# Cross attention: turning the probabilities in 32x32 blocks on VectorE and through DRAM, with the gather two batches later

## What is computed

```python
def _L0_xattn_ref(x, z, Wq, Wkv, Wo):        # x: 64 x 32 x 512 (after a layernorm), z: 64 x 257 x 256
    Q = (x @ Wq.T).reshape(B, xN, NUM_HEADS, HEAD_DIM)
    KV = (z @ Wkv.T).reshape(B, zN, 2, NUM_HEADS, HEAD_DIM)
    K = KV[:, :, 0]
    V = KV[:, :, 1]
    attn = jnp.einsum('bqhd,bkhd->bhqk', Q, K) * SCALE
    attn = jax.nn.softmax(attn, axis=-1)
    O = jnp.einsum('bhqk,bkhd->bqhd', attn, V).reshape(B, xN, DIM)
    return O @ Wo.T
...
x = x + _L0_xattn_ref(_layernorm(x, axis=-1), ctx_512, ...)
x = x + _L0_attn_ref(_layernorm(x, axis=-1), ...)
x = x + _L0_ffn_ref(_layernorm(x, axis=-1), ...)
```

## Time and profile before

| | us |
|---|---|
| three timed runs | 1493.66, 1495.41, 1495.46 |
| median | 1495.41 |
| span of the profiled execution | 1492.9 |
| loop of the cross attention within it | from 32.2 to 687 |

### The profile page before, as it was taken

One profiled execution on the slowest core, in us unless ns is written; L12 is line 12 of the kernel. 1 busy time (PEld: TensorE's weight loads), 2 busy tenths in 40 slices (PEclk: granted clock), 3 DMA queues, 4 the chain that ended last, 5 costly groups with the idle time before them and its releaser, 6 DMA issues. The chain is left out here.

```text
span 1492.9 us, 39481 instructions
## 1 busy us (share of the span) xinstructions
PE 1434.5 (96%) x14944; PEld 1281.3 (86%) x14944; DVE 1088.6 (73%) x1945; ACT 807.5 (54%) x1525; POOL 543.6 (36%) x810
## 2 busy tenths in 40 slices
PE   7999999999999999998999998799999999999998
PEld 6888888988888888887778786698999999999997
DVE  3676777767777677776667686797887878787785
ACT  4666666666666666654434434345555545555452
POOL 1222222221222222224866876453333333333232
PEclk9999999999999999999999999899999999999999
DMA  6301101000001100100011014179877878787871
GB/s 239 125 28 31 30 22 29 29 22 29 22 28 28 29 28 23 30 9 1 31 38 38 32 38 155 57 220 314 281 263 247 286 253 267 262 279 238 292 256 44
DMA packets 130734, 174.11 MB, mean 117 GB/s; under 512 B 16953, under 2 KB 89337, under 8 KB 130626
## 3 DMA queue, kind: packets, MB, share of 16 engines
q1 hardware_dynamic: 120242, 145.56, 30.1%
q0 software_dynamic: 10384, 27.05, 5.0%
HBM read 157.18 MB, written 19.06 MB: 118 GB/s over the span
## 5 line engine op out<-in xcount | busy, mean ns | idle before, releaser
L2229 DVE TENSOR_TENSOR split<-raw,split 128x1024 fp32r<-128x1024 f32 x204 | 242.3, 1220 | 7.2 <-ACT split L2169 6.0
L52 PE MATMUL bank<-split_xT,split 128*128 128x256 f32 x768 | 216.5, 282 | 0.4 <-DVE split L2229 0.2
L54 PE MATMUL bank<-split_xT,split 128*128 128x256 f32 x768 | 215.4, 281 | 0.0
L53 PE MATMUL bank<-split_xT,split 128*128 128x256 f32 x768 | 215.4, 280 | 0.0
L2169 ACT CAST split<-raw 128x1024 fp32r<-128x1024 f32 x202 | 203.2, 1048 | 6.9 <-DMA raw<-in_L_ffn_W_dram 3.2
L596 ACT ACTIVATE Pr<-xa_s,nmax 128x257 f32<-128x257 f32 x256 | 118.7, 473 | 124.9 <-DVE nmax L696 124.8
L2189 ACT ACTIVATE sl<-bank 128x256 f32<-128x256 f32 x115 | 44.2, 384 | 240.8 <-PE bank L54 223.5
L52 PE MATMUL xa_s<-split,split 128*128 128x258 f32 x512 | 150.5, 294 | 1.9 <-DVE split L628 1.9
L52 PEld LDWEIGHTS bank<-split_xT,split 128*128 128x128 f32 x768 | 144.9, 189 | 7.0 <-issue 2.8
L53 PEld LDWEIGHTS bank<-split_xT,split 128*128 128x128 f32 x768 | 145.0, 189 | 3.1
L53 PE MATMUL xa_s<-split,split 128*128 128x258 f32 x512 | 145.6, 284 | 0.0
(11 more groups left out here) (317 smaller groups left out, 3915.1 us busy)
## 6 DMA issues: line engine op xcount, KB each, us to landing
raw<-in_L_ffn_W_dram SPq DMA_DIRECT2D x207, 512.0 KB
raw<-in_ctx_dram SPq DMA_DIRECT2D x64, 256.0 KB, 2.6
out_dram<-x_res SPq DMA_DIRECT2D x16, 256.0 KB
xs<-xn SPq DMA_DIRECT2D x16, 256.0 KB
x_res<-in_x_dram SPq DMA_DIRECT2D x1, 3584.0 KB, 18.7
VL<-v_last_rows SPq DMA_DIRECT2D x128, 2.0 KB, 1.5
raw_o<-in_L_xattn_Wo_dram SPq DMA_DIRECT2D x1, 1024.0 KB, 6.4
raw_q<-in_L_xattn_Wq_dram SPq DMA_DIRECT2D x1, 1024.0 KB, 9.5
```

Source lines behind the costliest of these rows:

```text
L52: pe.matmul(out, lh, rh, start=start, stop=False)
L53: pe.matmul(out, ll, rh, start=False, stop=False)
L54: return pe.matmul(out, lh, rl, start=False, stop=stop)
L2229: vW.done(dve.tensor_tensor(lo, raw, hi.bitcast(F32), ALU.subtract), f"p{c}{q}")
```

## The change

The probabilities are no longer turned by TensorE (but for the very last batch). VectorE transposes them in blocks of 32x32 within the partitions, in two instructions (`turn_blocks`). SP stores the result to a DRAM scratch of 128 x 1024 floats (`put`) and loads it back with another assignment of rows to partitions (`meet`), which makes the blocks meet in the right partitions. `pt_hi` now splits 1024 columns from SBUF in one pass of ScalarE, and `pt_lo` is a pass of GpSimd instead of two of VectorE. The gather stands two batches behind the scores instead of one. The scores may now use all four banks as soon as the exponentials have read them. On TensorE the once-a-tile work moves by a batch. The scratch, the turned block and the met block exist once each: `turn_blocks` waits for the store and load of the batch before. The context load of a later batch stands between `put` and `meet`, and waits for `pt_lo`. The load of `wo`, whose buffer the turned blocks use, comes after the loop. GpSimd's wait for `qk_lo` is gone.

```diff
+
+        P_turned, P_met = (spare_p.w13[:, n].rearrange("p k w -> p (k w)") for n in range(2))
+        turned_blocks = P_turned.rearrange("p (b c m q) -> p c m b q", b=BT, c=CH, m=NQ)
+        put_dram, met_dram = turned_dram, turned_dram.rearrange("(r i) (b e) -> (i b) r e", r=HEADS, b=BT)
...
+                def ask_z(s, j):
+                    sp.wait_ge(pe_T, s - BT + 1)
+                    sp.wait_ge(g_Z, s - BT + 1)
+                    sp.wait_ge(g_PT, s - BT + 1)
+                    load_z(sp, s, j)
+
+                def put(s):
+                    sp.wait_ge(v_TP, CH * s + CH)
+                    sp.dma_start(put_dram, P_turned).then_inc(p_put, 16)
+
+                def meet(s):
+                    sp.wait_ge(p_put, 16 * s + 16)
+                    sp.dma_start(P_met.rearrange("p (r e) -> p r e", r=HEADS), met_dram).then_inc(p_met, 16)
+
                 def tile(i, u, first, last, more):
-                    for j in range(BT):
-                        s = BT * i + j
...
                         weights.load(sp)
+                    for j in range(BT):
...
+                            last_values(i)
+                        if last and j == BT - 1:
+                            return
+                        put(s)
+                        if last and j > 0:
+                            sp.wait_ge(g_PT, s)
+                        elif not (first and j == 0):
+                            ask_z(s + BT - 1, (j + BT - 1) % BT)
+                        meet(s)
                 by_pair(sp, tile)
+                sp.wait_ge(a_PT, s_end - 1)
+                sp.wait_ge(g_PT, s_end - 1)
+                weights.load_last(sp)
 
...
@@ -423,24 +455,27 @@
                     pe.wait_ge(g_L, s + 1)
                     pe.wait_ge(v_QK, s + 1)
                     for m in range(NQ):
-                        if some and m >= 2:
-                            pe.wait_ge(v_PT, 2 * s + m - 3)
+                        if some:
+                            pe.wait_ge(a_E, 4 * s + m - 3)
                         for k in range(KL):
                             mm = product(pe, bank_s[:, m, 0:KW], (QK_hi[:, k, m * P:(m + 1) * P], QK_lo[:, k, m * P:(m + 1) * P]),
                                          (zT_hi[:, k, :], zT_lo[:, k, :]), k == 0, k == KL - 1)
                         mm.then_inc(pe_S, 1)
 
-                def gather_z(s):
+                def gather_z(s, z, probs):
 
                     pe.wait_ge(g_Z, s + 1)
-                    pe.wait_ge(v_PT, 2 * s + 2)
                     need(pe, U_out, s)
                     for k in range(KL):
                         for c in range(CH):
-                            mm = product(pe, bank_u[:, k],
-                                         (zn_hi[:, c, k * P:(k + 1) * P], zn_lo[:, c, k * P:(k + 1) * P]),
-                                         (PT_hi[:, c, :], PT_lo[:, c, :]), c == 0, c == CH - 1)
+                            mm = product(pe, bank_u[:, k].rearrange("p (r e) -> p r e", r=HEADS),
+                                         tuple(n[:, c, k * P:(k + 1) * P] for n in z),
+                                         tuple(n[:, :, c, :] for n in probs), c == 0, c == CH - 1)
                     mm.then_inc(pe_U, 1)
+
+                def gather_met(s):
+                    pe.wait_ge(g_PT, s + 1)
+                    gather_z(s, zn, PT)
...
-                        if j == 0 and not first:
+                        if not first or j >= 2:
+                            gather_met(s - 2)
+                        if j == 1 and not first:
                             last_values(i - 1)
-                        if j == 2 and not last:
+                        if j == BT - 1 and not last:
                             need(pe, v_OP, i)
...
-                        if j == 0 and not first:
+                        if j == 0 and not first and (more or u == 0):
+                            project_q(i + 1, 1)
+                        if j == 1 and not first:
                             values(i - 1)
-                        if j == 1 and not first:
+                        if j == 2 and not first:
                             project_o(i - 1)
-                        if j == 2 and more:
+                        if j == BT - 1 and more:
                             project_q(i + 2, 0)
-                        if j == 3 and more:
-                            project_q(i + 2, 1)
                         if step is not None:
                             pe.wait_ge(a_QK, step[3])
-                        turn_p(s)
...
                 def pt_hi(s):
+                    act.wait_ge(p_met, 16 * s + 16)
+                    need(act, pe_U, s)
+                    act.copy(PT_hi.rearrange(by_head), P_met).then_inc(a_PT, 1)
...
@@ -591,31 +636,40 @@
                         for m in range(NQ):
                             act.wait_ge(v_mx, 2 * s + m // 2 + 1)
                             if m == 0:
-                                need(act, pe_PT, 2 * s)
+                                need(act, v_TP, CH * s)
                                 need(act, v_R, s)
                             act.activation(Pr[:, m, 0:NK], bank_s[:, m, 0:NK], ACT.Exp, bias=nmax[:, m:m + 1],
                                            scale=1.0, accum_out=rsum[:, m:m + 1]).then_inc(a_E, 1)
                         if not (last and j == BT - 1):
                             t = u if j < BT - 1 else 1 - u
                             qk_hi(s + 1, t, (j + 1) % BT, BT * i + (BT if j < BT - 1 else 2 * BT))
-                        if j == 2 and not last:
+                        if j == BT - 1 and not last:
                             x_out(act, i + 2)
+                        if j == 1 and not first:
+                            u_out(s - 2, BT - 1)
+                        if j % 2 == 0 and not (first and j == 0):
+                            pt_hi(s - 1)
                         if not (last and j == BT - 1):
                             z_hi(s + 1)
+                        if j % 2 == 1:
+                            pt_hi(s - 1)
                         if step is not None:
                             act.wait_ge(v_QK, s + 1)
                             for n in range(2):
                                 qk_out(step[3] - 2 + n, step[0], step[1] + n)
-                        if j > 0:
-                            u_out(s - 1, j - 1)
-                        if j == 0 and not first:
+                        if j >= 2:
+                            u_out(s - 2, j - 2)
+                        if j == 0 and not first and (more or u == 0):
+                            q_out(i + 1, 1 - u, (1,))
+                        if j == 1 and not first:
                             ot_hi(i - 1)
-                        pt_hi(s)
-                        if j >= 2 and more:
-                            q_out(i + 2, u, (j - 2,))
+                        if j == BT - 1 and more:
+                            q_out(i + 2, u, (0,))
                 by_pair(act, tile)
...
+                def turn_blocks(s):
+                    need(dve, p_put, 16 * s)
+                    need(dve, p_met, 16 * s)
+                    dve.wait_ge(v_N, s + 1)
                     for c in range(CH):
-                        dve.wait_ge(a_PT, 2 * s + c + 1)
-                        dve.tensor_tensor(PT_lo[:, c, :], bank_pt[c], PT_hi[:, c, :].bitcast(F32), ALU.subtract
-                                          ).then_inc(v_PT, 1)
+                        dve.transpose(turned_blocks[:, c], Pr[:, :, c * P:(c + 1) * P].rearrange("p m (i b) -> p m b i", b=BT)
+                                      ).then_inc(v_TP, 1)
+
...
-                        if j == 0 and not first:
-                            u_out(s - 1, BT - 1)
                         if not (last and j == BT - 1):
                             qk_lo(s + 1, u if j < BT - 1 else 1 - u, (j + 1) % BT)
                             z_lo(s + 1)
+                            turn_blocks(s)
+                        if j == 0 and not first:
+                            u_out(s - 2, BT - 2)
                         if j == 1:
                             if first:
                                 dve.wait_ge(x_rest, 16)
                             statistics(dve, i + 2)
-                        if j == 0 and not first:
+                        if j == 1 and not first:
                             ot_lo(i - 1)
-                        if last and j == BT - 1:
+                        if j == 2 and not first:
+                            add_residual(i - 1)
+                        if j == BT - 1:
                             last_weights(i)
-                        pt_lo(s)
-                        if j == BT - 1 and not last:
-                            last_weights(i)
-                        if j == 1 and not first:
-                            add_residual(i - 1)
...
-                def split_z(s, j, i):
+                def split_z(s, j, i, z=zn):
+                    hi, lo = z
```

(23 more changed lines are left out.)

77 lines of the change are left out of this document (50 added, 27 removed).

## The result

| | kernel before | changed kernel |
|---|---|---|
| median of four runs, us | 1494.54 | 1543.31 |
| lowest and highest | 1493.13 to 1495.46 | 1541.65 to 1546.88 |
| span of the profiled execution | 1492.9 | 1539.9 |

The ratio is 1.0324, with a 95% interval of 1.0304 to 1.0343. The forecast was 1485, a gain of 0.7%; the measured time lies above its range too.

What follows compares the result with a forecast made beforehand. TensorE, 96% busy, bound the old kernel; the new chain of 19.73 us a pair made 39.6 a tile against 40.39, 11 us over 14 tiles, net 10 after the ends: 1485 us, likeliest 1470 to 1497, whole range 1450 to 1520.

Steps and rivals of the forecast that it cites:

- The sum: Chain through an odd batch and the even one behind it (a pair), scores to next odd scores: 19.73 us.
- 1.34 us: VectorE's two block transposes a batch, priced from self attention's 711 ns row, the second following after about 0.63.
- break-even: Two batches took 20.2 us before; a round trip of 6.7 us instead of 6.3 would make the change even.
- The rival on strides: Block transposes reading every fourth float cost 0.34 us more per 512 columns; 1496 us, no change; chance 0.15.
- GpSimd's lateness: GpSimd's low part ends late and delays issue of the load: 0.2 us a pair, 0.25 more for context packets.
- The round trip: Store to DRAM 2.6, load back 3.4 and handing over 0.3: 6.3 us, on the path in even batches.
- 0.3 for handing over: Allowance added to the store's 2.6 and the load's 3.4 us in the round trip.
- 0.8 for pieces of 1 KB: Addition to 3.6 us that gave the load's upper bound of 4.4 us; 3.4 was taken.
- The third rival: Store and load take longer than 6.3 us; 56 us at the upper bounds, 1513 with half; chance 0.30.
- The port: GpSimd and VectorE passes over SBUF exclude one another, so GpSimd's context split begins only 7.6 us into the batch.
- The clock: TensorE resting some 1.5 us in even batches might drop to half clock, adding up to 2.9 us a scores stage.
- The ends of the loop: First two batches save about 2 us without gathers; two gathers behind a last round trip cost about 3 more.

Runs made afterwards that it cites:

- plain_read: Changed kernel with block transposes reading 32 neighbouring columns instead of every fourth one, probabilities ending in another order: 1513.3 us.
- permuted: Changed kernel with the stride moved to the splits that read PSUM, so block transposes read neighbouring columns and the result is the same: 1518.0 us.
- half_load: Changed kernel with the load from DRAM bringing half of the block (256 KB), the other half staying from the first batch: 1512.7 us.
- keep_wait: Changed kernel with GpSimd's wait for the split of QK put back before it splits the context: 1535.7 us.
- the late pass: Changed kernel with ScalarE's pass over the loaded probabilities in even batches moved behind the context and absorbed-key copies: 1501.0 us.
- direct: Changed kernel without DRAM scratch, four DMAs taking the turned blocks straight to their places in SBUF: 1532.2 us.
- absorb_twice: Changed kernel with TensorE doing the absorption of the keys twice in each even batch, same result: 1543.8 us.
- no_round_trip: Changed kernel with store and load issued for the first batch alone, later passes rereading that block (output wrong): 1498.4 us.

## Why the prediction was wrong

**The mechanism was right, the block transposes were mis-sized.** The sum said 8.20 + 1.34 + 6.3 + 0.45 + 1.02 + 0.49 + 1.93 = 19.73 a pair. Measured from the rows above: 8.40 until the context split ends; 2.09 for the transposes; 6.74 from their end to the pass; 3.36 for the pass, context copy and key copies; and 0.33 from the end of the key copies to the first matmul, which the sum left out: 20.92.

The step that failed is "1.34 us" for two block transposes, taken from the one of self attention; this one reads every fourth column and takes 1.10, which is 0.75 a pair, 1.5 a tile, 21 us. The break-even stood at 20.2 a pair: this term alone, put right in the sum, turns the sign (19.73 + 0.75 = 20.48). plain_read and permuted showed its size by taking it away.

They showed as well that it isn't all. With the transposes at their forecast price a pair of plain_read still takes 9.14 + 11.03 = 20.17 us, not 19.73, most of it the 0.33 left out; the steady loop is level with the kernel before, and with what the ends cost, 1513 is still 17 us slower. So the forecast gain was lost without the stride too; the stride is the largest single term, not the sole one.

**The rival on strides had the mechanism and half of the price.** It took 0.34 per 512 columns from the earlier trace rows, two rows that differ in what they write as well as in the step (32 results and 4), and let GpSimd's lateness cover part, and so came to "no change". Measured are 0.42 per 512 columns (1.10 and 0.68), and nothing was covered. The rule of the Trainium skill on two hits per 16-byte line (SBUF — State Buffer, "Specifications") pointed the right way: the trace agrees for this read of SBUF (1.10 for 0.68), and says nothing of why. No loss was seen where PSUM was read by the same step (permuted).

**The round trip was as long as forecast, in other parts.** 6.74 against 6.3 + 0.45. From the transposes' end to the issue of the load passed 2.65 (2.6 forecast for the store); the load landed in 4.0 instead of 3.4; GpSimd's pass, which was to hold the load up, ended 1.3 us before it was issued. No row stood behind the 0.3 for handing over and the 0.8 for pieces of 1 KB; here SP issued the store 0.03 us after the transposes, and ScalarE's pass began 4.09 after the issue of the load. half_load gives the load's size: 1.1 us for 256 KB, 0.4 more than the earlier trace rows let expect; that the pieces of 1 KB are the reason wasn't tested. The third rival, a longer round trip, gave the right side and at its upper bounds nearly the right size (1485 + 56). That is luck, but for the clock, which it named: the round trip was no longer than summed, and the loss came from the transposes, the hand-over and the ends.

**The port.** GpSimd's conversion met VectorE's passes as forecast (1.61 us instead of 0.61), but keep_wait shows that this decided little in the changed kernel. Where it decides is VectorE's delay in the batch with j = 0 once the late pass has taken the round trip off the path (2.29 us for 1.22 in the split of QK), which the forecast had not.

**The clock** was named as a risk and not in the sum: five steady tiles lost 1.5 us each, 7.6 us. All its low batches with j = 1 followed rests of 2.0 to 2.3 us, but so did most of the full ones. In the steady tiles of the other profiles it came five times in direct (rests like those of the changed kernel), three times in absorb_twice, twice in half_load and keep_wait, once in plain_read and permuted, and never in the five kernels with the late pass or without the round trip, whose rests before the scores with j = 1 were 0.1 to 1.4 us. What decides it stays open.

**The ends of the loop were mis-sized.** Forecast was a loss of 1 us, measured 2.6 + 13.4 = 16. The last tile's three batches took 33.65 us for 28.44, and then comes the tail:

```profile
713.76 0.79 PE L52 MATMUL xa_u<-split,split_xT 128*128 128x512 f32 x1 [4.44 <-POOL split L822]
...
719.51 0.47 PE L52 MATMUL xa_u<-split,split_xT 128*128 128x512 f32 x1 [1.07 <-ACT U L617]
...
727.13 0.47 PE L52 MATMUL xa_o<-split,split_xT 128*128 128x512 f32 x1 [1.52 <-DVE split_xT L737]
```

The gather of the last but one batch waits 4.44 us for the last round trip and GpSimd, starts at the lower clock, and the last gather, the values and the output projection come behind it. From the last scores to self attention there are 30.3 us, before 22.0 (665.46 to 687.48). 7.9 of the 8.3 us more have passed when the last gather starts; the waits behind it, the 1.52 us among them, are those of the kernel before. Even no_round_trip, faster by 0.6 us in each steady tile, is no faster than the kernel before as a whole.

Behind the forecast, then: 57 us between the spans = 32 in the steady chain (21 of them the stride, 9 the hand-over of 0.33) + 8 clock + 15 at the ends + 2 to 3 behind the loop. The stride's share is shown by runs that take it away; the hand-over, the clock and the ends are read from the traces.

## What to carry to other kernels

When a new instruction borrows its price from a row, compare the access pattern as well as the size: a step of four in the operand made a transpose 1.6 times as long, and moving the step to the passes that read PSUM made it free in this loop. When work is taken off a saturated engine, list in what order each other engine's queue releases the next round, and keep the instruction that waits for the longest transfer behind everything that does: one place in ScalarE's list was worth 42 us here, the transposes' stride another 22 behind it. Price the first and the last round of a deeper pipeline by themselves.

## What the runs showed of the hardware

- A block transpose of 128x512 on VectorE takes 1.10 us when it reads every fourth float of SBUF and 0.68 when it reads neighbours. ScalarE and VectorE passes of 512 columns that read PSUM by every fourth float took 0.59 and 0.69, as with neighbours.
- 512 KB stored to DRAM in rows of 4 KB landed in 2.6 us, 2.9 beside another load; 512 KB loaded in pieces of 1 KB in 3.9 to 4.0, 256 KB of it in 2.9.
- A DMA from SBUF to SBUF with 128 KB took SP 0.6 us to issue, where one between SBUF and DRAM took 0.33 to 0.37.
- A GpSimd pass over SBUF that stood waiting during one VectorE pass had its turn before the next one and held that up to its own end (2.29 us for 1.22). A GpSimd pass that met VectorE's took 1.61 instead of 0.61. In both the waiting shows as a longer duration of the instruction that waits.
- TensorE's granted clock was 0.50 for 3 us in the scores behind a rest of 2.21 us; behind other rests of 1.8 to 2.9 us it stayed full.
- 0.33 us passed from the end of a ScalarE copy to the first matmul that waited for it.
